# A mixture-of-experts kernel on one core: the weighted sum of four expert results laid over quarters of the partitions

## The reference, cut to what matters

```python
scores = jnp.sqrt(jax.nn.softplus(flat @ router_w.T))
_, idx = jax.lax.top_k(scores + expert_bias, 4)
topv = jnp.take_along_axis(scores, idx, axis=1)
topv = topv / (topv.sum(axis=-1, keepdims=True) + 1e-20)
probs = jnp.zeros((T, 32)).at[jnp.arange(T)[:, None], idx].set(topv)
# for each expert e, over all 2048 tokens:
acc = acc + probs[:, e][:, None] * clamped_swiglu(flat, gate_w[e], up_w[e], down_w[e])
out = acc + clamped_swiglu(flat, shared_gate_w, shared_up_w, shared_down_w)
x = x + out
```

## Time and profile before

| what | value |
|---|---|
| median of 3 runs | 691.42 us (689.58 to 693.4) |
| profiled execution, its own time | 689.39 us |
| its span, first to last instruction | 687.6 us |
| mean granted clock of TensorE | 0.965 of full speed |
| busy: PE, DVE, ACT, POOL | 592.0, 442.0, 391.8, 373.1 us |
| HBM read, written | 53.92 MB, 100.28 MB |

### The profile page before, as it was taken

One profiled execution on the slowest core, in us unless ns is written; L12 is line 12 of the kernel. 1 busy time (PEld: TensorE's weight loads), 2 busy tenths in 40 slices (PEclk: granted clock), 3 DMA queues, 4 the chain that ended last, 5 costly groups with the idle time before them and its releaser, 6 DMA issues.

```text
span 687.6 us, 14458 instructions
## 1 busy us (share of the span) xinstructions
PE 592.0 (86%) x4117; PEld 476.3 (69%) x4117; DVE 442.0 (64%) x1374; ACT 391.8 (57%) x1156; POOL 373.1 (54%) x527
## 2 busy tenths in 40 slices
PE   0588899999998899998899778785887999999985
PEld 0488777787776688777686556553666887788863
DVE  1546656777666876757756586276655777655576
ACT  1002366766777655784657886662534666677660
POOL 6837847457455565586735434614154555555560
PEclk9999999999999999999999999896789999999999
DMA  7989999999999996123323965876443555555599
GB/s 261 263 210 335 335 334 334 332 330 324 318 311 324 317 304 209 52 59 113 118 71 110 347 208 156 275 266 211 147 125 108 163 157 162 149 164 161 158 349 345
DMA packets 130204, 155.02 MB, mean 225 GB/s; under 512 B 15216, under 2 KB 117744, under 8 KB 129744
## 3 DMA queue, kind: packets, MB, share of 16 engines
q1 hardware_dynamic: 112000, 122.50, 59.0%
q0 software_dynamic: 7632, 20.98, 8.5%
q10 hardware_dynamic: 10496, 10.62, 4.9%
HBM read 53.92 MB, written 100.28 MB: 224 GB/s over the span
## 4 chain that ended last, share of the span: by engine, by line
PE 62%; DVE 13%; POOL 7%; ACT 7%; issue 6%; DMA 3%; another core or an unknown queue 1%; SPq 1%; ACTq 0%; DVEq 0%; POOLq 0%
PE ps L416 11%; PE pc L679 11%; PE pS L383 6%; PE pS L659 4%; POOL arena L1441 4%; PE ps L461 3%; PE ps L645 2%; PE po L630 2%; PE ps L488 2%; PE ps L522 2%; PE po L406 2%; PE ps L514 2%; PE ps L505 2%; PE ps L591 2%; DMA arena<-y_rows 2%
## 5 line engine op out<-in xcount | busy, mean ns | idle before, releaser
L679 PE MATMUL pc<-arena,tk 128*128 128x128 f32 x768 | 109.5, 296 | 13.3 <-POOL arena L1441 7.2
L679 PEld LDWEIGHTS pc<-arena,tk 128*128 128x128 f32 x768 | 97.7, 203 | 25.5 <-issue 13.3
L416 PE MATMUL ps<-arena,work 128*128 x380 | 102.2, 393 | 1.4 <-ACT work L1193 1.4
L1441 POOL TENSOR_TENSOR arena<-arena 128x512 f32<-128x512 f32 x64 | 90.2, 1423 | 21.8 <-ACT arena L1239 21.6
L1455 POOL DMA_INDIRECT expert_rows<-stage,ixl x64 | 63.6, 994 | 37.0 <-DVE ixl L1056 19.4
L1306 ACT ACTIVATE work<-pS,work 128x128 f32<-128x128 f32 x256 | 72.5, 369 | 4.4 <-DVE work L958 4.0
L416 PEld LDWEIGHTS ps<-arena,work 128*128 128x128 f32 x380 | 67.5, 198 | 7.5 <-issue 1.8
L755 DVE TENSOR_SCALAR work<-ps 128x256 f32<-128x256 f32 x95 | 40.1, 422 | 46.5 <-PE ps L416 44.7
L383 PE MATMUL pS<-arena,tk 128*128 x190 | 61.1, 404 | 8.1 <-ACT tk L1188 6.5
L1183 ACT ACTIVATE tk<-work 128x128 f32<-128x128 f32 x95 | 29.4, 310 | 57.7 <-DVE work L755 48.6
L958 DVE TENSOR_REDUCE work<-pS 128x4 f32<-128x512 f32 x64 | 43.9, 685 | 24.6 <-PE pS L659 21.3
(11 more groups left out here) (317 smaller groups left out, 1463.8 us busy)
## 6 DMA issues: line engine op xcount, KB each, us to landing
expert_rows<-stage SPq DMA_DIRECT2D x32, 2080.0 KB, 20.7
work<-expert_rows SPq DMA_DIRECT2D x95, 130.0 KB
arena<-in_w SPq DMA_DIRECT2D x16, 768.0 KB
stage<-xn_rows SPq DMA_DIRECT2D x64, 130.0 KB
xn_rows<-xnD ACTq DMA_DIRECT2D x16, 512.0 KB, 4.9
arena<-y_rows SPq DMA_DIRECT2D x8, 512.0 KB, 9.9
tk<-in_tk SPq DMA_DIRECT2D x1, 2048.0 KB, 10.0
work<-y_rows SPq DMA_DIRECT2D x4, 512.0 KB
```

Source lines behind the costliest of these rows:

```text
L416: i = pe.matmul(p[U * k:U * k + U, 0:256], xgT[n % 3][:, 128 * c + U * k:128 * c + U * k + U], arena[:, 256 * c:][:, bass.ds(e, 256)], sta ...
L679: i = pe.matmul(pv, tk[:, h, 128 * d:128 * d + 128], kvv[:, ci, :, :].rearrange("p b (i h j) -> p (b i) h j", i=8, h=8)[:, :, hl, :], star ...
L1441: pool.tensor_tensor(kv[kk % 4][:, c, half, :].rearrange("p (i h j) -> p i h j", h=8, i=8), i0, i1, ALU.mult).then_inc(s_kv, 1)
```

## The change

- **Places of the choices.** Each choice k gets the 32 partitions from 32 k on. A group g of four batches has a place `ranks[g]` of 128 x 4096 values: partition 32 k + p holds, for j = 0..3 and four batches, the result rows of choice k of token 32 j + p. Four loads per choice, 512 KB each, fill them, each into 32 partitions.
- **Sum.** For each batch one matrix `mixes[b]` (128 x 128) holds the four choices' weights, spread over a folded identity; for each j one multiplication with its 32 columns j sums over all four choices at once, onto 32 partitions of the accumulator. All 16 batches go this way; a bank holds two batches, and DVE adds a bank at a time.
- **Weights.** DVE moves `pk4` into the new layout in loop ticks 57 to 60 (16 narrow copies) and builds the 16 mixes in ticks 62 to 77. ACT's diagonals go.
- **Row loads.** DVE copies column 256 of each tile's rows to column 257 (after waiting for the landed scatter of tile n - 12), and the scatter reads its places there. The row load brings columns 0 to 256 only and waits for that copy (`s_ix`), not for the landed scatter.
- **Result loads.** All four choices go to places that are free once 79 tiles are multiplied (`gone[16]` of the worst case); no load waits for the last tile.

```diff
+        gone = [EARLY + (NB * 128 * KT - EARLY * U + e * (U - 1)) // U for e in range(NE)]
+        ranks = [m.rearrange("p (j b d) -> p j b d", j=4, b=4)
+                 for m in (work[:, WORK - 4096:WORK], *(arena[:, 4096 * g:4096 * g + 4096] for g in range(3)))]
+        fold = score[:, 0, 0:NE]
+        pT = lg[0][:, 0:64].rearrange("p (b j) -> p b j", j=4)
...
+            pe.wait_ge(s_y, NT)
             pe.wait_ge(s_acc, NB)
-            def weigh(c, k, b):
...
+            for b in range(NB):
+                p = accs[b // 2]
+                if b % 4 == 0:
+                    pe.wait_ge(d_in[2 + b // 4], 48 + 16 * KT)
+                pe.wait_ge(s_dg, b + 1)
+                for j in range(4):
+                    i = pe.matmul(p[32 * j:32 * j + 32, 256 * (b % 2):256 * (b % 2) + 256], mixes[b][:, 32 * j:32 * j + 32],
+                                  ranks[b // 4][:, j, b % 4, :], start=True, stop=True)
...
                     dve.tensor_tensor(th[n % 3][:, 1, :], cl[n % 3][:, 0:128], cl[n % 3][:, 128:256],
                                       ALU.mult).then_inc(s_m, 1)
+                    if n >= NX:
+                        dve.wait_ge(d_y[(n - NX) % 4], 16 * ((n - NX) // 4 + 1))
+                    dve.wait_ge(d_g[n % 4], 16 * (n // 4 + 1))
+                    dve.tensor_copy(xg[n % NX][:, 257:258].bitcast(I32), xg[n % NX][:, 256:257].bitcast(I32)).then_inc(s_ix, 1)
...
+                for k in at(t, 57, 1, KT):
+                    for j in range(4):
+                        dve.tensor_copy(pT[32 * k:32 * k + 32, :, j], pk4[32 * j:32 * j + 32, :, k]).then_inc(*own.up())
+                    dve.wait_ge(*own.now())
+                for b in at(t, 62, 1, NB):
+                    if b >= 12:
+                        dve.wait_ge(d_sc[b - 12], 16 * SC[b - 12])
+                    dve.tensor_tensor(mixes[b].rearrange("p (j c) -> p j c", j=4), fold.unsqueeze(1).broadcast_to((128, 4, 32)),
+                                      pT[:, b, :].unsqueeze(2).broadcast_to((128, 4, 32)), ALU.mult).then_inc(s_dg, 1)
...
-            def weigh(k, b):
...
+            for n in range(NB // 2):
+                dve.wait_ge(s_yp, NT + n + 1)
+                dve.tensor_tensor(xs[:, 2 * n:2 * n + 2, :], accs[n][:, :].rearrange("p (b d) -> p b d", b=2),
+                                  xs[:, 2 * n:2 * n + 2, :], ALU.add).then_inc(s_acc, 1)
...
             def result_steps(n):
+                pool.wait_ge(s_ix, n + 1)
                 pool.wait_ge(s_y, n + 1)
...
                     if n >= NX:
-                        sp.wait_ge(d_y[(n - NX) % 4], 16 * ((n - NX) // 4 + 1))
+                        sp.wait_ge(s_ix, n - NX + 1)
                     r = sp.snap(half[n - n0], min_val=0, max_val=NE * NB * 128 + 384)
-                    sp.dma_start(xg[n % NX], Xs[bass.ds(r, U), 0:260]).then_inc(d_g[n % 4], 16)
+                    sp.dma_start(xg[n % NX][:, 0:257], Xs[bass.ds(r, U), 0:257]).then_inc(d_g[n % 4], 16)
...
                 if k == KT - 1:
                     sp.wait_ge(s_acc, NB)
+                    sp.wait_ge(s_yp, gone[16])
                 sp.wait_ge(s_st, last[k])
                 sp.sem_inc(s_thr, 1)
-                yk = Yr[DUMP + NB * 128 * k:DUMP + NB * 128 * (k + 1), :].rearrange("(p b) d -> p b d", b=NB)
-                if k == 2:
-                    sp.wait_ge(s_yp, GONE3)
...
-                if k == 1:
-                    sp.wait_ge(s_yp, NT)
-                    continue
+                yk = Yr[DUMP + NB * 128 * k:DUMP + NB * 128 * (k + 1), :].rearrange("(j p b) d -> p j (b d)", j=4, b=NB)
                 for g in range(4):
...
+                    sp.dma_start(ranks[g][32 * k:32 * k + 32, :, :, :].rearrange("p j b d -> p j (b d)"),
+                                 yk[:, :, 1024 * g:1024 * g + 1024]).then_inc(d_in[2 + g], 16)
```

More of the change, by code:

```diff
@@ L63 @@
 DUMP = 512
[L64 to L73, removed]
 NX = 12
@@ L248, in build @@
         stage = sb("stage", [128, NS, ROW])
[L250 to L255, removed]
-            if k == 2:
-                n = [n for n, (b0, b1, p) in enumerate(PIECES) if b0 <= b < b1][0]
-                return PIECES[n][2][:, b - PIECES[n][0], :], (d_in[n], 64)
-            g = b // 4
-            if k == 1:
[L261 to L264, removed]
+        mixes = [*(m[:, 4 * n:4 * n + 4, :].rearrange("p b e -> p (b e)") for m in (lg4, Sall, Ball) for n in range(4)),
+                 *(stage[:, n, 0:128] for n in range(4))]
+        gone = [EARLY + (NB * 128 * KT - EARLY * U + e * (U - 1)) // U for e in range(NE)]
[3 more added lines that the diff above has]
+        pT = lg[0][:, 0:64].rearrange("p (b j) -> p b j", j=4)
         carve = cutter(tk[:, 6:8, :].rearrange("p a b -> p (a b)"))
@@ L333, in build @@
         gbanks, xbanks, ybanks = banks.tiles[0:2], [banks.tiles[3], cbanks.tiles[0]], sbanks.tiles
+        accs = [*gbanks, *xbanks, po, banks.tiles[2], *ybanks]
         place = banks.place
@@ L688, in tensor_program @@
             pe.wait_ge(s_hT, NT)
-            accs = [*gbanks, *xbanks, po, banks.tiles[2]]
+            pe.wait_ge(s_y, NT)
             pe.wait_ge(s_acc, NB)
-            def weigh(c, k, b):
[L692 to L696, removed]
-                    i.then_inc(s_yp, 1)
[L699 to L704, removed]
+            for b in range(NB):
[6 more added lines that the diff above has]
+                                  ranks[b // 4][:, j, b % 4, :], start=True, stop=True)
+                if b % 2:
+                    i.then_inc(s_yp, 1)
         def vector_program(dve):
@@ L1173, in tile_steps @@
             def tile_steps(t):
[L1174 to L1177, removed]
-                    act.activation(diag[c], ident, ACT.Copy, scale=pk4[:, b, k:k + 1]).then_inc(s_dg, 1)
                 for n in at(t, 2, 1, NT):
@@ L1355, in scalar_program @@
                     tile_steps(i)
-            for c in range(2 * NPS, KT * NPS):
-                b, k = ENDP[(c - 2 * NPS) // 2], 1 - c % 2
-                act.activation(diag[c], ident, ACT.Copy, scale=pk4[:, b, k:k + 1]).then_inc(s_dg, 1)
             act.wait_ge(s_st, NT - 4)
@@ L1377, in result_steps @@
             def result_steps(n):
+                pool.wait_ge(s_ix, n + 1)
                 pool.wait_ge(s_y, n + 1)
                 pool.indirect_dma_start(
[L1380 removed]
+                    out=Yr, out_offset=bass.IndirectOffsetOnAxis(ap=xg[n % NX][:, 257:258].bitcast(U32), axis=0),
                     in_=y[n % NY], in_offset=None).then_inc(d_y[n % 4], 16)
```

48 lines of the change are left out of this document (11 added, 37 removed).

## The result

Median 702.21 us of four runs (697.27 to 704.82), beside 690.57 of four runs of the kernel before (689.58 to 693.4): ratio 1.0177 [1.0116, 1.0239], so 8 to 17 us slower. The forecast was 697.6 within 687 to 708.

The account below looks back on a forecast made before the run. TensorE was taken to bound the tile loop, result loads and the weighted sum the end. The tail's +4.7 us and index copies' 1.5 gave +6.2 us, 697.6 on the median, range 687 to 708.

Parts of the forecast that it names:

- The case forecast: Result loads beside the last scatters: half-speed loads hold scatters, delaying the end; +6.2 us with smaller parts, chance 0.58.
- The price without a row: Speed of result loads into 32 partitions: taken as half, 210 GB/s, between 105 and 420.
- Rival 1: Result loads beside the last 16 scatters: loads into 32 partitions run at full speed; 688.3 us, chance 0.25.
- Rival 2: Loop end and loads: half-speed loads, but scatters not held; 693.1 us, chance 0.12.
- Rival 3: Result loads: a quarter of the speed; 745 us on the median, chance 0.05.
- the clock's drop: Last tiles: TensorE, busy only 60%, might fall to the lower clock, with the end near 706.
- pieces and rows take turns one for one: Result loads beside scatters: 128 load pieces alternate with a scatter's 128 rows, 2.0 us per turn before the change.
- S: Time of one turn of load pieces and scatter rows in the tail: 2.0 us before, 2.7 forecast.
- the first decides: End: weighing after tile 94's copy ends at 688.9, the load-bound path at 687.6, so the copy's path sets the end.
- my lower bound: Weighing: at least 0.43 us per batch of four multiplications; 0.6 was taken, 9.6 us for 16 batches.
- The smaller parts: Tile loop: index copies 1.5 us (bounds 0 and 3.2); mixes and narrow copies covered by idle time, else 4.6 + 2.7.
- signs named: Profile after: last row load near 642, scatters 2.7 us apart, weighing about 10 us, no load waits before its last group.

Follow-up runs that it names:

- e2: Changed kernel with all result loads waiting until the last tile is multiplied; 726.42 us, ratio 1.0505.
- e1: Changed kernel with each result load (same bytes) writing 128 partitions instead of 32, output not the layer's; 691.52 us, ratio 1.0011.
- e9: Changed kernel with each choice on 32 partitions four apart, weights reordered through memory instead of narrow copies, mixes from tile 66; 686.41 us, ratio 0.9974.
- e12: Changed kernel without the row-load part: no index copy, row loads wait for landed scatters again; 702.61 us, ratio 1.0202.
- e6: Changed kernel with 64 result loads of 128 KB, by group, then j, quarters in the order 0, 2, 1, 3; 694.32 us, ratio 1.0089.
- e7: e6 without the row-load part: no index copies, row loads wait for landed scatters again; 694.6 us, ratio 1.0108.
- e10: e9 with the 95 index copies moved from DVE to POOL; 685.33 us, ratio 0.9940.
- e11: Kernel before with the row-load part alone: index copy on DVE, row loads wait for that copy; 694.28 us, ratio 1.0097.
- e5: Changed kernel with each result load writing 64 neighbouring partitions instead of 32, output not the layer's; 698.57 us, ratio 1.0141.
- e8: Changed kernel with the 16 narrow copies and the mixes behind them three tiles later; 698.85 us, ratio 1.0139.
- e3: Changed kernel with loads by group, each of 16 loads writing all four partition quarters at once; 749.3 us, ratio 1.0853.

## Why the prediction was right, and what was mis-sized

**The mechanism held, but for which path ends last.** The case forecast (loads into 32 partitions at half speed, the last scatters held by them, the end later) is what happened. The price without a row, half of 420 GB/s, was a middle taken between two ends, and e2 measured it alone: 200 to 204. By the ratio of 0.58 at 1 MiB in the Trainium skill, "SBUF — State Buffer" (Door 1: The DMA port swizzle), the loads would have had 242 GB/s; e2 has 0.48 to 0.49, nearer to my middle value. The 420 that I took for loads alone hold the end of the scatters too (queue q0 moved 0.07 of 2.10 MB from 675 to 680), which changes the half by a few per cent only.

**Rival 1, full speed,** gave a tail 4.6 us shorter than before; where e1 and e9 give the loads the full rate, their tails are 5.7 and 7.4 shorter. So its sum was sound to 1 to 3 us, and its condition did not hold. **Rival 2** (scatters not held) falls: copy 94 starts 8.2 us later against tile 80. **Rival 3** falls with the rate. Of the clock's drop the end felt 1.7 us, in the first part of the weighing (3.64 against 1.93 in e9).

**The size, term by term, against the profiled spans:**

| term | forecast | found |
|---|---|---|
| ahead of the tile loop | 0 | +4.9 (scatter) |
| tile loop to tile 80 (index copies) | +1.5 | +2.2 |
| tail from tile 80 | +4.7 | +7.1 |
| sum | +6.2 | +14.2 |

Between the medians it is +11.6. In the tail, counted from tile 80's copy (643.94 forecast, 651.05 found):

- *First load*: forecast 1.9 us ahead of it, found 0.8 ahead. The absolute 642 was 8 us off mostly because the loop ran 7.1 later.
- *The step that failed* is "pieces and rows take turns one for one", with one S for loads and scatters. Scatters took 2.27 us each, under my 2.7; loads took more: group 0 has its last load, the 13th, at 689.09, 38.9 us behind the first, 2.99 each. Before, both had 2.0; a load had half as much again, a scatter little more.
- So "the first decides" was wrong as well: I let the weighing start behind tile 94's copy (at 35.0 behind tile 80's, the weighing at 35.4) and group 0's 13 loads come in ahead of it (13 S from 642, at 33.2). Found: that copy at 31.0, the loads and the weighing at 38.0, 2.7 later than the start forecast. The scatters came 4.0 earlier and the loads 4.8 later than forecast; that the tail came out as near as it did is partly luck.
- *From there to the end*: forecast 13.0 (9.6 + 0.68 + 2.7), found 12.7 (701.8 - 689.09). The weighing took 9.2 us to the 9.6 forecast, in spite of half the clock in its first part; at full clock a batch is 0.43 (0.86 per bank of two), my lower bound.
- 2.7 - 0.3 is the 2.4 that the tail has over the forecast.

**The smaller parts.** The index copies, with their waits, cost 1.2 to 2.2 us from tile 12 to 80 (2.9 in the changed kernel against 1.3 in e12, 3.0 in e6 against 1.3 in e7, 2.7 in e9 against 1.5 in e10, 2.2 in e11), some 0.9 of it at the one place where all kernels stand still, so not by the score sums alone; the size is near my 1.5. Narrow copies: tiles 53 to 56 add 0.4 (1.7 in e5, and in e8, where they come later), against 0.2 in e9 without them; mixes: tiles 56 to 80 add 0.2 (1.3 in e8, where the narrow copies are among them). In the changed kernel both are near the nothing that I wrote. Of the signs named, the eight additions (0.69), the 128 records (9.2 us) and ACT's waits for landings were there; the wait for loads stood before the first group, not the last, which is the failed step above. DVE's wait for landed scatters did not show in the loop.

## What to carry to other kernels

Before a layout gives each of several loads its own block of partitions, ask which partitions each load writes: neighbours halved the rate here (254 to 264 GB/s beside scatters, 200 to 204 alone, of 420), the same number of partitions four apart kept it (397 to 413 beside scatters), and that, with the weights brought into the same order, turned 1.8% slower into the kernel before's time. A rate read beside other traffic holds that traffic's bytes too; measure the disputed transfer alone. And start loads earlier only where their end is what the kernel waits for: alone the earlier start cost 1.0%, beside the slow loads it earned its price.

## What the runs showed of the hardware that I had not expected

- The rate of a load depends on which partitions it writes and not on their number: 32 neighbours 254 to 264 GB/s, 64 neighbours 261, 32 four apart 397 to 413, all 128 417, each with the bytes of the scatters beside it.
- A load whose source has an outermost dimension of 4 took a quarter of the engines' time and ran at 103 GB/s (e3).
- One small copy per tile, 0.15 us on an engine that was idle 23% of the loop before (15.32 busy of 20), was not free: it cost 1.2 to 2.2 us between tiles 12 and 80, some 0.9 of it at one place near tile 52 where DVE or ACT stood still in all fourteen profiles, with nothing to wait for that the profile shows.
